# Graph network kernel on one core: the last stage's stores on two queues, four adds on GpSimd, two maxima on ScalarE, and two branches on TensorE where there were ten

## The reference

```python
h = jnp.maximum(_layernorm(x, axis=-1), 0.0)
x = x + _L0_gnn_ref(h, bases, w_comp, h_bias, edge_weight1, src, dst, edge_type_32)   # relational layer
h = jnp.maximum(_layernorm(x, axis=-1), 0.0)
x = x + _L1_gnn_ref(h, edge_index, W, b)

def _L1_gnn_ref(x, edge_index, W, b):
    row = concatenate([edge_index[0], loops]); col = concatenate([edge_index[1], loops])
    deg = segment_sum(ones(row.shape[0]), row); dis = rsqrt(deg)
    norm = dis[row] * dis[col]
    h = x @ W.T + b
    out = segment_sum(norm[:, None] * h[row], col)
    return relu(out)
```

## Time and profile before

| | us |
|---|---|
| median of 3 runs | 613.32 |
| lowest and highest run | 612.7, 614.57 |
| the profiled execution's own time | 613.97 |
| its span in the trace | 612.2 |
| TensorE busy | 494.9 (81%) |
| VectorE busy | 348.6 (57%) |
| GpSimd busy | 355.9 (58%) |
| ScalarE busy | 155.9 (25%) |

### The profile page before, as it was taken

The page is one execution under the profiler, slowest core; times in us unless marked ns, Lnnn a source line. Parts: engine busy times, 40 slices in busy tenths (PEclk is TensorE's granted clock), DMA queues, the critical chain, the costliest instruction groups (busy, mean ns, idle before and its releaser), DMA issues.

```text
span 612.2 us, 16075 instructions
## 1 busy us (share of the span) xinstructions
PE 494.9 (81%) x5905; PEld 314.5 (51%) x5905; DVE 348.6 (57%) x1007; ACT 155.9 (25%) x280; POOL 355.9 (58%) x476
## 2 busy tenths in 40 slices
PE   3041552889998999999699998898989998999973
PEld 1031542556566666656456556555656565664530
DVE  8983788575663456746655666653666324232035
ACT  3674546222220122310220320220323101122020
POOL 3636668555767776757457757657767777730000
PEclk9665765799999999999799999898999999999985
DMA  8789995565886877867566857858867878855016
GB/s 281 234 282 393 393 303 147 150 199 162 258 253 197 277 230 214 273 203 214 178 181 183 252 168 229 258 156 240 266 205 221 277 234 254 237 150 155 0 27 144
DMA packets 51957, 132.84 MB, mean 217 GB/s; under 512 B 11791, under 2 KB 17792, under 8 KB 51718
## 3 DMA queue, kind: packets, MB, share of 16 engines
q0 software_dynamic: 27040, 99.60, 53.9%
q1 hardware_dynamic: 23884, 30.99, 16.2%
q10 hardware_dynamic: 954, 1.13, 0.6%
HBM read 123.14 MB, written 11.10 MB: 219 GB/s over the span
## 4 chain that ended last, share of the span: by engine, by line
PE 59%; DVE 16%; DMA 11%; issue 5%; ACT 4%; POOL 2%; SPq 1%; DVEq 0%; ACTq 0%
PE PS L1713 26%; PE PS L1691 19%; DMA gath<-rows_layer,srcs 10%; PE PS L1754 6%; PE PS L1733 4%; POOL gath L784 2%; DVE room_b L1338 2%; DVE room_b L1381 2%; DVE zt L1338 2%; PE PS L1697 1%; DMA room_b<-in_L_gnn_bases_dram 1%; ACT room_b L924 1%; PE PS L1561 1%; ACT room_b L913 1%; DVE room_b L1530 1%
## 5 line engine op out<-in xcount | busy, mean ns | idle before, releaser
L784 POOL DMA_INDIRECT gath<-rows_layer,srcs x335 | 336.1, 1003 | 170.5 <-PE PS L1697 94.5
L1691 PE MATMUL PS<-sel,gath 128*128 128x48 f16 (+7 forms) x4020 | 312.8, 206 | 48.0 <-DVE zt L1338 14.3
L1691 PEld LDWEIGHTS PS<-sel,gath 128*128 128x128 f16 x4020 | 243.3, 102 | 171.8 <-issue 80.2
L1713 PE MATMUL PS<-room_b,zt 128*128 128x512 f16 x480 | 165.3, 391 | 0.0
L1713 PE MATMUL PS<-room_b 128*128 128x512 f16 (+1 forms) x480 | 149.5, 380 | 0.8 <-DMA gath<-rows_layer,srcs 0.4
L1697 PE MATMUL PS<-oh_ad,gath 128*128 128x30 bf16 (+7 forms) x335 | 64.6, 193 | 0.0
L1250 DVE TENSOR_TENSOR masks<-iota_n,dloc 128x24 bf16<-128x24 f32 (+12 forms) x92 | 17.9, 194 | 81.4 <-PE PS L1697 43.1
L1754 PE MATMUL PS<-u_t,room_c 128*128 128x512 f16 (+2 forms) x200 | 58.0, 399 | 6.1 <-issue 3.7
L1713 PEld LDWEIGHTS PS<-room_b 128*128 128x128 f16 (+1 forms) x480 | 47.3, 104 | 14.4 <-issue 0.6
L853 ACT CAST val<-val_f 128x64 f16<-128x64 f32 x42 | 11.0, 261 | 170.1 <-DVE val_f L1219 169.9
L1713 PEld LDWEIGHTS PS<-room_b,zt 128*128 128x128 f16 x480 | 45.6, 100 | 4.6
(11 more groups left out here) (237 smaller groups left out, 425.3 us busy)
## 6 DMA issues: line engine op xcount, KB each, us to landing
room_b<-in_L_gnn_bases_dram SPq DMA_DIRECT2D x8, 1024.0 KB, 12.0
gath<-rows_layer,srcs POOLq DMA_INDIRECT x335
x_t<-x_base SPq DMA_DIRECT2D x19, 128.0 KB
u_t<-in_x_dram SPq DMA_DIRECT2D x9, 256.0 KB, 6.5
x_base<-in_x_dram SPq DMA_DIRECT2D x9, 256.0 KB, 14.6
x_layer<-x_t SPq DMA_DIRECT2D x18, 128.0 KB, 3.9
gath<-x_layer SPq DMA_DIRECT2D x18, 128.0 KB, 2.7
out_dram<-gath SPq DMA_DIRECT2D x18, 128.0 KB
```

The lines of the kernel that those rows point to most:

```text
L784: pool.indirect_dma_start(out=gath[:, s % UN, :], out_offset=None, in_=tab0_d[:, :], in_offset=bass.IndirectOffsetOnAxis(ap=srcs[:, s:s + ...
L1691: mm(there, gath[:, s % UN, D * t + P * f:D * t + P * (f + 1)], sel_parts[:, here, k, 0:NB * w, u], start=first and t == 0 and u == 1, sto ...
L1713: last = mm(PS[0:r, PBANK[q], :], zt[q % 2][:, t, f, b, 0:r], base_hl[:, b, u, f, :], start=(m == 0), stop=(m == NM - 1))
```

## The change

It changes what the engines do after u of the last block exists; the two PE lines before that are the same.

- TensorE issues the high matmuls of positions 0 to 7 as one group once `s_uhi` is there, takes its branch, waits for `s_uev`, and issues the eight low matmuls. Then the same for positions 8 and 9. The two bodies now hold 320 and 80 matmuls.
- ScalarE also takes the maximum for positions 3 and 6, in place in `out_tmp`, and issues the second half's store of every block.
- GpSimd adds x1 for positions 0, 1, 3 and 6 (`PTAIL`) and counts them in `s_resp`.
- VectorE keeps `add_begun` for positions 2 to 9 and the combined maximum and add (now `larger`) for 2, 4, 5, 7, 8 and 9.
- SyncE's queue stores the first half of every block.
- `out_tmp` has ten places where it had eight.

```diff
+    PTAIL = [0, 1, 3, 6]
...
+        def store(eng, t, half):
+            if t in PTAIL:
+                eng.wait_ge(s_resp, PTAIL.index(t) + 1)
+            else:
+                eng.wait_ge(s_res, t + 1 - sum(p < t for p in PTAIL))
+            d, n, p = halves(TAIL[t])[half]
+            eng.dma_start(out[d:d + n, :], final(TAIL[t])[p:p + n, :]).then_inc(s_out, 16)
...
-            return room_b[:, D * (i % 8):D * (i % 8 + 1)]
+            return room_b[:, D * (i if i < 8 else i + 26):D * ((i if i < 8 else i + 26) + 1)]
...
-            for t, i in enumerate(TAIL):
-                sp.wait_ge(s_res, t + 1)
-                for d, n, p in halves(i):
-                    sp.dma_start(out[d:d + n, :], final(i)[p:p + n, :]).then_inc(s_out, 16)
+            for t in range(NT):
+                store(sp, t, 0)
             sp.wait_ge(s_out, 32 * NT)
...
+            pool.wait_ge(s_back, 32 * QL)
+            for n, t in enumerate(PTAIL):
+                x1 = final(TAIL[t])[0:ROWS[TAIL[t]], :]
+                pool.wait_ge(s_relu, n + 1)
+                g.tensor_tensor(x1, out_tmp(t)[0:ROWS[TAIL[t]], :], x1, ALU.add).then_inc(s_resp, 1)
...
+            sent = 0
+            for t in PTAIL[2:]:
+                while sent < t - 2:
+                    store(act, sent, 1)
+                    sent += 1
+                act.wait_ge(s_sum, t - 1)
+                there = out_tmp(t)[0:ROWS[TAIL[t]], :]
+                a.activation(there, there, ACT.Relu).then_inc(s_relu, 1)
+            for t in range(sent, NT):
+                store(act, t, 1)
...
-            add_x1(0)
-            add_x1(1)
+            dve.wait_ge(s_back, 32 * QL)
             add_begun(2)
             for t in range(3, NT):
                 add_begun(t)
-                add_x1(t - 1)
-            add_x1(NT - 1)
+                if t - 1 not in PTAIL:
+                    larger(t - 1)
+            larger(NT - 1)
...
+            for group in (range(0, 8), range(8, NT)):
+                for n in group:
+                    if n == 0:
+                        pe.wait_ge(s_uhi, NT)
+                    elif n == 6:
+                        pe.wait_ge(s_ub, NT)
+                    elif n == 7:
+                        pe.wait_ge(s_x1, NT)
+                    elif n >= 8:
+                        pe.wait_ge(s_relu, n - 7)
+                    spread(TAIL[n], QL, 0, C, FBANK[n], n >= 2 and n - 2 not in late)
                 with pe.If(any_order > 0):
...
+                if 0 in group:
+                    pe.wait_ge(s_uev, NT)
+                for n in group:
+                    spread(TAIL[n], QL, 1, C, FBANK[n], False).then_inc(s_fin, 1)
```

More of the change, by code:

```diff
@@ L516, in gnn_kernel @@
         s_res = sem("s_res")
+        s_resp = sem("s_resp")
         s_out = sem("s_out")
@@ L1531, in add_begun, with larger @@
                                        ALU.mult, ALU.add).then_inc(s_sum, 1)
-            def add_x1(t):
+            def larger(t):
                 j = TAIL[t]
[L1535 to L1544, removed]
-            add_x1(0)
-            add_x1(1)
+                x1 = final(j)[0:ROWS[j], :]
+                dve.wait_ge(s_sum, t - 1)
+                v.scalar_tensor_tensor(x1, out_tmp(t)[0:ROWS[j], :], 0.0, x1, ALU.max, ALU.add).then_inc(s_res, 1)
+            dve.wait_ge(s_back, 32 * QL)
             add_begun(2)
@@ L1816, in _ @@
             project(QL)
[L1817 to L1825, removed]
-                spread(j, QL, 0, C, FBANK[n], n >= 2 and n - 2 not in late)
+            for group in (range(0, 8), range(8, NT)):
[9 more added lines that the diff above has]
+                    spread(TAIL[n], QL, 0, C, FBANK[n], n >= 2 and n - 2 not in late)
                 with pe.If(any_order > 0):
                     pe.wait_ge(s_cext, 32)
-                    for q in range(NT):
-                        for t in range(2):
-                            for k in range(2):
-                                spread(j, q, t, k, FBANK[n], False)
-                spread(j, QL, 1, C, FBANK[n], False).then_inc(s_fin, 1)
+                    pe.wait_ge(s_uev, NT)
+                    for n in group:
+                        for q in range(NT):
+                            for t in range(2):
+                                for k in range(2):
+                                    spread(TAIL[n], q, t, k, FBANK[n], False)
+                if 0 in group:
+                    pe.wait_ge(s_uev, NT)
+                for n in group:
+                    spread(TAIL[n], QL, 1, C, FBANK[n], False).then_inc(s_fin, 1)
 _INS = ['x', 'src', 'dst', 'edge_type_32', 'edge_weight1', 'L0_gnn_bases', 'L0_gnn_w_comp', 'L0_gnn_h_bias',
```

## The result

The changed kernel takes **611.23 us** in the median of 8 runs (609.47 to 613.05), and the kernel before 614.57 in the median of 7 on the same chips. Two runs far slower than the rest are left out of every comparison here, one of the kernel before (2701.35 us) and one of the changed kernel in the group with early_branch (687.21 us). The ratio of the means is 0.9946, with a 95% interval of 0.9919 to 0.9972, so it is faster by 3.3 us, with 1.7 to 5.0 as the ends. The forecast was 611.1, with 2.2 us less. That 611.1 comes so near is partly luck, because the kernel before ran 1.3 us longer beside it than in the runs shown earlier. The difference is what has to be explained.

A forecast was written before the change was run, and what follows sets the result against it. The prediction took the store stream, finishing later than VectorE, as the bound: 19.5 stores at 0.58 us from 597.8 end at 609.1 instead of 611.3. Taking 2.2 us from 613.32 gave 611.1 us, range 608.6 to 613.8.

The forecast's parts named there:

- What bounds the end: Last stage: VectorE at 1.26 us per block and the store stream at about 1.3 run in parallel; the stream finishes late.
- TensorE: Last stage: long branch at 591.2 costs 3.0 us, low matmuls start at 594.2, 0.43 us each; second branch costs nothing.
- The slower rival: TensorE's long branch costs 6.2 us and stores keep 0.64 us each: 615.5 us, a loss; chance 0.08.
- VectorE: Last stage: 14 instructions take 8.9 us, from 595.7 to 604.6, ending 1.0 us earlier than before.
- The rival in which GpSimd and VectorE block each other: Each of GpSimd's four adds holds VectorE for its whole 1.16 us: 613.5 us; chance 0.07.
- GpSimd's adds: Adds of x1 in the last stage: likeliest 1.16 us each, from above twice that; first stores issued at 596.7.
- The store stream: Output stores at the end: 19.5 at 0.58 us each, 11.3 us, from 597.8 to 609.1 instead of 611.3.
- side by side: Store halves move unhindered on two queues, so VectorE's pace decides: 3.8 to 4.7 us less, 609.2; chance 0.33.
- The two held issues: SyncE's store issues of 1.81 and 1.77 us, where 0.60 is usual, disappear; some 2.4 us were lost there.
- The range: Whole kernel's time: from 608.6, side by side without any delay, to 613.8, a little above the blocked case.
- The signs: Changed profile: branch about 3 us, low matmuls from 594.2, first store 596.7, DMA share near 1.0 at 225 GB/s without gaps.
- keeps its pace: Store stream stays at 0.64 us per store from 597.8, ending at 610.3: 1.0 us less, 612.3; chance 0.15.

The follow-up runs named there:

- early_branch: Changed kernel with TensorE's long branch moved behind the last projection, and a short branch for the high matmuls: median 609.97 us, ratio to before 0.9937.
- split_only: Kernel before with only the stores shared, first halves on SyncE's queue and second halves on ScalarE's: 611.29 us against 614.35, ratio 0.9947.
- one_queue: Changed kernel with all 20 stores on SyncE's queue: 614.70 us against 613.53 for the kernel before, ratio 1.0033.
- burst_low_high: Changed kernel with all stores held until everything is computed, then lower halves on SyncE's queue, upper on ScalarE's: 9.9 us from first to last byte.
- early_and_order: early_branch with TensorE's matmuls regrouped (positions 0 to 2, then 3 to 7) and VectorE's maxima placed away from GpSimd's adds: ratio to before 0.9951.
- pool_memset: Changed kernel with GpSimd writing zeros instead of its four adds: one run, 16.6 us from ScalarE's last high half to the span's end.
- pe_undone: Changed kernel with TensorE's tail of the kernel before, ten branches: ratio to before 0.9962.
- the bursts: Three variants of the changed kernel with all stores held until everything is computed: 9.9 us (opposite halves), 12.3 (same half), 12.7 (one queue).

## Why the prediction was right and where it failed

**What bounds the end**, two processes in parallel of which the store stream is the late one: right for the kernel before. split_only shows it best, since nothing but the stores was changed there: VectorE ended later and the span earlier.

**TensorE**: right in sum, by two errors that cancel. The branch takes 3.52 us instead of 3.0, but starts right at H and not 0.7 us later, so the low matmuls begin at H + 3.65 where the forecast had H + 3.7. After that the matmuls take 0.23 us each (ten in 2.33) instead of 0.43. Their PEclk wasn't at half, as I had taken from the earlier trace rows: the window from 592.80 to 595.20 shows 1.00, and it is at 0.50 only in the window from 599.00 on. So VectorE starts at H + 4.6, 0.6 earlier than forecast. This differs from one execution to the next. In one_queue, where TensorE has the same work, the low matmuls did run at 0.50 (timeline and window):

```profile
597.28 4.97 PE L1768 MATMUL PS<-u_t,room_c 98*128 98x512 f16 x12 [1.71 <-issue]
```

```profile
597.20:601.60 4.40, 4.32 (x11) 1.62 (x12) 2.75 (x3) 1.90 (x3) 2.84 (x3) 0.50 0.12 27
```

There a matmul took 0.43 us, and VectorE began at H + 5.5. The second branch (1.23 us, from 594.6) is covered, as costed at nothing. The Trainium skill, Runtime: NRT & Kernel Launch, "Instruction fetch mechanics", says that a taken branch out of the loaded two pages forces a fetch before execution goes on; the 3.52 us agree with it. The slower rival needed over 4.0 us.

**VectorE**: the count of 14 instructions was right, the 8.9 us weren't. It took 10.1 us, from 593.78 to 603.92, and 1.0 of the 1.2 us more is the one instruction of 1.67; most of the rest is one of 0.82. Its end was put at H + 14.1 and came at 14.7. The rival in which GpSimd and VectorE block each other was there, at about a quarter of its price, because only one of four adds met a combined instruction in full.

**GpSimd's adds** take 1.27 us where I took 1.16, and once 1.73 beside VectorE; the bounds were 1.16 and 2.3. First stores at H + 6.2 and first bytes at H + 7.4, forecast 6.2 and 7.3.

**The store stream is the step that failed.** I took 0.58 us for each store, one after another, 11.3 us in all, with an end at H + 18.6. It took 10.1 us and ended at H + 17.5. With nothing else in its way the same stream takes 9.9 us, 0.51 per store (burst_low_high), so the price was too high by 0.07 us per store. In the changed kernel it is paced by VectorE, with its lag of 2.8 us. The mechanism is that of the rival "side by side", which had 0.33 and promised 3.8 to 4.7 us (its earliest end, 606.4, is 4.9 before 611.3). It gives less than that for two reasons with a number each: the halves together reach 260 to 294 GB/s and not 400, and VectorE is held. The two held issues are nearly gone, as forecast: the longest of SyncE's queue is 1.17 us.

**The range** was right: 611.23 lies in it, and 3.3 us is above the 1.84 us that can be told from no change. **The signs** were right for the branch, the start of the low matmuls and the first stores. For the stores I had named a DMA share near 1.0 at 225 GB/s without gaps, and had called the forecast wrong if they weren't back to back. The share is 0.90 at 294 GB/s and 0.84 at 269, with 0.61 at 148 in the window from 596.60, and the queues wait for results between stores. By that sign the store stream of the forecast was wrong, and the sign of the blocked rival, a VectorE instruction well over 0.75 us, did appear. So the direction and the range came true while the main term worked by another mechanism than the one I had priced. That the time came near the forecast all the same is partly luck: 3.3 us lies between my 2.2 and the rival's 3.8 to 4.7.

What stays open is why two halves together give 302 GB/s of busy DMA engines and not the 386 (405/1.05) of the earlier trace rows, and why the last bytes land 2.5 to 3.0 us after VectorE's end even with the split, where issue, start and one pair of stores make about 1.8. I didn't try one transfer of all 128 partitions per block; the kernel uses two, because the halves are two separate pieces of the output.

The rival "keeps its pace" has a reading that doesn't come out: the late start of 3.0 us is more than the 2.4 us of the held issues, and not half of them. What makes the difference is that the old stream also waited for results. From first to last byte it took 16.5 us where 19.5 stores at 0.64 take 12.5, so 1.6 us of waiting stand beside the 2.4.

## What to carry to other kernels

Look at the partitions that each store reads before counting queues: in the bursts two queues gained 28% on different halves and 3% on the same half. Read what comes after the last engine's end: VectorE's end moved by 0.4 us and the time by 3.3. The long branch took 3.3 to 3.9 us wherever it stood, so put it where the engine waits anyway, and when work moves to GpSimd, price what its instructions do to VectorE's beside them that read two operands from SBUF.

## What the hardware showed that I had not expected

- Two queues with stores of 64 partitions: 260 GB/s on opposite halves, 208 on the same half, 202 on one queue.
- A combined VectorE instruction of 0.68 us took 1.67 beside one GpSimd add and 2.86 behind two that followed each other; GpSimd let nothing in between the two. The other way round, GpSimd's add took 1.73 instead of 1.27, and 2.24 beside two combined instructions in a row (early_and_order).
- The long branch over 320 matmuls took 3.3 us (pool_memset) to 3.9 us (early_and_order) with idle DMA engines. Those over 40 matmuls that stood still took 2.5 us (pe_undone) to 3.4 us (split_only), beside stores. The second branch of the changed kernel, over 80, took 1.23 us. So the time didn't go by the distance here.
- The granted clock stayed at 1.00 (2.4 GHz) for the changed kernel's low matmuls after standstills of 1.66 and 1.70 us, 0.23 us each. In one_queue, with the same TensorE work and standstills of 1.66 and 1.71 us, it fell to 0.50 (1.2 GHz) at H + 1.6, and twelve matmuls took 4.97 us. Before, TensorE had been idle for 2.45 us ahead of 591.36, the clock fell at H + 1.8, and six matmuls took 2.74 us. So the length of the standstill ahead of the work doesn't tell by itself at which level it runs.
